# Attention and routing of the second layer in two halves: row sends begin while the second half is still in attention, shared products in waits, and sixteen products of the identity

## The chip, the cores and the metric

The kernel runs on one core of one Trainium2 chip. The metric is the device time of one execution in microseconds (us). Engines are named as in the profile: PE (TensorE), DVE (VectorE), ACT (ScalarE), POOL (GpSimd), SP (SyncE, which issues transfers).

## The reference, cut to what matters

x and ctx hold 8 blocks of 128 tokens with 256 values. Two layers follow one another; each adds an attention and a routed feed-forward network to x. The change concerns what lies between the first network and the second.

```python
h = layernorm(x)                                   # layer 1, attention
theta = theta_w @ ctx; phi, g = phi_w @ h, g_w @ h # 64 latent rows per block
t = softmax(theta^T phi) weighs g                  # 256 x 256 scores per block
z = layernorm over all 64 x 256 values of t, times ln_gamma, plus ln_beta
x = x + ctx + out_w @ relu(z) + out_b

h = layernorm(x)                                   # layer 1, network: 32 experts, top 6
scores = sigmoid(h @ gate_w.T)                     # 8 groups of 4 experts, best 4 groups allowed
idx = top_k(masked scores, 6); w = scores[idx] / sum * 2.5
y = sum over k of w_k * expert_idx_k(h)            # silu(h w11) * (h w33) @ w22
x = x + y + shared(h)                              # one expert twice as wide, for every token
```

Layer 0 has a long convolution as its attention and a network of 8 experts, top 2.

## The kernel before

**Tiling.** All 1024 tokens lie in SBUF as 8 blocks of 128 partitions x 256 values (`x_sb`, normalised `h_sb`, turned `hT_hi` and `hT_lo`, which together hold full precision). Each engine runs its own program; the order of the work is written out by hand in it, and semaphores join them. There is no planner.

**Attention of layer 1.** PE makes theta, phi and g of all blocks, then per block `scores`, `turn_probs` (turning the 256 x 256 probabilities) and `weigh`. DVE takes row maxima (`row_max`, L1301), divides by the sums (`normalise`, L1306 and L1308) and takes statistics of `tx` (L1314). ACT makes the exponentials. The norm over 64 x 256 values goes by groups of four blocks: averages over partitions on PE (`means`, `spreads`), `variance` on DVE, the power -0.5 on POOL (L705), `shifts` on DVE (L1341), scale and shift on ACT; gamma and beta are applied on POOL for blocks 0 to 3 (L711, L717) and on DVE for blocks 4 to 7 (`affine`, L1350, L1352). `outputs` multiplies by out_w, `add_out` (L1360) adds to x.

**Routing of layer 1.** After layer norm 3 of all eight blocks (`veps` L956, power on POOL L588, `shift` L962, normalised rows L976 on DVE and L743 on ACT), PE turns the rows (L1444), makes the logits by expert in eight products of 512 columns (L1454), which ACT copies and PE turns back (L1461). DVE copies scores (L1087), ACT takes the sigmoid, DVE picks groups and experts for all eight blocks (L1092 to L1121). POOL ranks each token's chosen experts by shift and add (`rank` L646, L651, `nth` L656); PE counts rows per expert; DVE makes slots (L1140 to L1153).

**Row sends.** Every token goes to six experts. For k = 0 to 5, DVE stages slots and gates of the k-th choice of all eight blocks (L1211 to L1221), and POOL sends one block of 128 rows at a time to a table `rows_s` in DRAM (L665, an indirect transfer, 48 in all). `staged` has three buffers, so from k = 3 on the staging waits until the sends of k - 3 have landed. POOL's program around it is

```python
pool.wait_ge(slots_made, n * TOPK[0] + k + 1)
for b in range(B):
    ...
    nc.gpsimd.indirect_dma_start(
```

**Experts of layer 1.** 32 chunks of 224 rows: SP loads `rowbuf` from `rows_s` (chunk c waits for the sends of k = 0 to min(c, 5)), PE turns it (L1524) and multiplies (L1431 to L1433, L1557), ACT writes `y_sb` (L840), POOL sends it to a second table `y_s` in two indirect transfers (L683, 64 in all). When these have landed, `y_s` is loaded and added to x, and x is written out. The shared expert's products (`shared_up`, `shared_down`) stand on PE behind the logits. Ahead of the first `turn_rows` PE waits for `add_banks` (L992), which DVE runs behind the last staging.

Of the kernel before, what the change touches and what calls it, by code (L numbers as in the profile page):

```python
# [6 lines left out]
P = 128  # L7
B, S, D = 8, 128, 256
# [41 lines left out]
def build(nc, x_d, ctx_d, ctxr_d, filt_d, skip_d, wr_d, up0_d, down0_d, theta_d, theta_b_d, phi_d, phi_b_d, g_d, g_b_d,  # L50
# [11 lines left out]
    with ExitStack() as stack:  # L62
# [39 lines left out]
        gates = [sb("gates0", [P, B, E0]), sb("gates1", [P, B, E1])]  # L102
        gsum = sb("gsum", [P, B])
        grec = sb("grec", [P, B])
        mask = sb("mask", [P, B, E1])
        rank = [sb(f"rank{i}", [P, B, 16 + E1]) for i in range(2)]
        nth = sb("nth", [P, B, E1])
        cum = [sb(f"cum{i}", [P, 4 + B, E1]) for i in range(2)]
        cend = [sb(f"cend{i}", [P, 16 + E1]) for i in range(2)]
        past = sb("past", [1, MAXC[1] + 2 - FIXED_CHUNKS[1], E1])  # L110
        before = sb("before", [P, P])
        ones = sb("ones", [P, P])
        slot_f = sb("slot_f", [P, B, E1])
        pick = [sb(f"pick{i}", [P, B, E1]) for i in range(2)]
        slot_k = sb("slot_k", [P, B])
        slot_i = sb("slot_i", [P, TOPK1, B], i32)
# [4 lines left out]
        ends_f = sb("ends_f", [1, E1])  # L121
# [31 lines left out]
        idle = sb("idle", [1, 4])  # L153
# [8 lines left out]
        shift2 = sb("shift2", [LAT, B])  # L162
# [55 lines left out]
        pool_made, dve_consts = sem("pool_made"), sem("dve_consts")  # L218
# [10 lines left out]
        lgT_done, lgT_copied, mask_made, ranked = sem("lgT_done"), sem("lgT_copied"), sem("mask_made"), sem("ranked")  # L229
        cum_made = sem("cum_made")  # L230
        nth_made, pool_step = sem("nth_made"), sem("pool_step")
        table_made, h_staged, slots_made = (sem(n) for n in ("table_made", "h_staged", "slots_made"))
        rows_sent = [sem(f"rows_sent{k}") for k in range(TOPK1)]
# [11 lines left out]
        class Ffn:  # L245
# [19 lines left out]
        mean_in, mean_done, dev_in, dev_done, var2_ready, rstd2_ready, shift_made = (sem(n) for n in (  # L265
            "mean_in", "mean_done", "dev_in", "dev_done", "var2_ready", "rstd2_ready", "shift_made"))
        zb_made2 = sem("zb_made2")
        z_made, zg_made, zb_made, relu_made, w_done, ctx_added = (sem(n) for n in (
            "z_made", "zg_made", "zb_made", "relu_made", "w_done", "ctx_added"))
# [62 lines left out]
        def wait_normed(eng, k, batches):  # L332

            eng.wait_ge(normed[1], 6 * k + min(batches, 4) + max(batches - 6, 0))
            if batches > 4:
                eng.wait_ge(normed[0], 2 * k + min(batches - 4, 2))
# [40 lines left out]
        SCORES = (4, 5, 0)  # L377
        OUT = (2, 3, 4, 5)

# [1361 lines left out]
```

## Time and profile before

| | before |
|---|---|
| median of 3 runs | 436.21 us (435.19 to 436.69) |
| the profiled execution's own time | 435.86 us |
| its span in the profile | 434.1 us |
| busy PE / DVE / ACT / POOL | 286.5 / 243.3 / 174.1 / 225.4 us |
| mean granted clock of PE | 0.82 |
| attention of layer 1 starts, about | 184.6 us |
| row sends of layer 1 | 263.9 to 326.8 us |
| y sends of layer 1 | 327.1 to 418.3 us |

The profile is of one execution, 1.76 us shorter in span than its own time. Clock figures are shares of 2.4 GHz, so 0.50 is 1.2 GHz. A timeline row is: start in us, duration in us, engine, line, operation, output <- inputs, shape, count, and in brackets the idle time ahead of it with what ended it.

### The profile page before, as it was taken

Reading aid. Unit: us, or ns where it says so; the run is one execution under the profiler, and the core shown is the slowest. Engines: PE = TensorE matmul, PEld = TensorE weight load, DVE = VectorE, ACT = ScalarE, POOL = GpSimd, SP = SyncE. Lnnn points to the kernel's source line nnn. Section 1 sums busy time; section 2 is a strip of 40 time slices with the busy share of each in tenths; the row PEclk is TensorE's granted clock in tenths of the full one; section 3 lists DMA queues with packets and bytes.
Section 4 is the critical chain, followed back from the end, with each engine's and each line's share of the span. In section 5 each row is a group of like instructions: output and inputs, shape, how many; then the busy total and the mean of one; then the engine's idle time right before and its main releaser. Section 6 shows DMA issues by size and latency. Waiting matters only on the chain.

```text
span 434.1 us, 5040 instructions
## 1 busy us (share of the span) xinstructions
PE 286.5 (66%) x1416; PEld 205.5 (47%) x1416; DVE 243.3 (56%) x659; ACT 174.1 (40%) x378; POOL 225.4 (52%) x253
## 2 busy tenths in 40 slices
PE   0899957202899993299927836621834899998800
PEld 0444433102798881065513524321734899997700
DVE  3599986721353432643667699515412476665467
ACT  2400005501456443254655661201412868886600
POOL 2578821177044654240064045777776667778840
PEclk9999985655999998595975887955866999999955
DMA  7566798424567514999933001343347955699499
GB/s 229 154 169 169 198 298 249 135 99 116 166 198 230 169 45 147 327 321 307 309 116 96 26 1 61 121 144 132 121 144 225 301 164 152 195 293 285 132 376 306
DMA packets 66062, 80.56 MB, mean 186 GB/s; under 512 B 7643, under 2 KB 55061, under 8 KB 66035
## 3 DMA queue, kind: packets, MB, share of 16 engines
q1 hardware_dynamic: 56547, 62.45, 48.9%
q0 software_dynamic: 7296, 16.93, 11.4%
q10 hardware_dynamic: 2192, 0.86, 0.8%
q8 instruction: 12, 0.20, 0.2%
q14 instruction: 15, 0.12, 0.1%
HBM read 43.70 MB, written 38.01 MB: 188 GB/s over the span
## 4 chain that ended last, share of the span: by engine, by line
PE 40%; POOL 18%; DVE 15%; DMA 11%; issue 11%; ACT 4%; SPq 0%; POOLq 0%; DVEq 0%
POOL rows_s L665 12%; PE banks L1557 6%; DMA y_s<-y_sb,place 4%; PE banks L1431 4%; PE banks L1412 3%; PE banks L1432 3%; PE banks L1433 3%; POOL y_s L683 3%; PE banks L1413 3%; PE banks L1414 3%; PE banks L1524 3%; PE banks L1444 2%; PE banks L1644 2%; PE banks L1624 2%; DMA staged<-y_s 2%
## 5 line engine op out<-in xcount | busy, mean ns | idle before, releaser
L683 POOL DMA_INDIRECT y_s<-y_sb,place x88 | 91.0, 1034 | 48.3 <-ACT y_sb L840 24.0
L665 POOL DMA_INDIRECT rows_s<-staged,slot_i x64 | 65.4, 1022 | 28.1 <-issue 27.8
L1431 PE MATMUL banks<-xT_hi,w_hi 128*128 128x224 f32 (+1 forms) x192 | 64.4, 335 | 4.8 <-DVE w_lo L1241 4.5
L1524 PE MATMUL banks<-ident,rowbuf 112*128 112x112 f32 (+1 forms) x176 | 25.7, 278 | 51.1 <-DMA rowbuf<-rows_s 35.6
L1432 PE MATMUL banks<-xT_lo,w_hi 128*128 128x224 f32 (+1 forms) x192 | 57.1, 297 | 0.0
L1433 PE MATMUL banks<-xT_hi,w_lo 128*128 128x224 f32 (+1 forms) x192 | 56.8, 296 | 0.0
L826 ACT ACTIVATE xT_hi<-banks 128x448 fp32r<-128x448 f32 (+1 forms) x40 | 22.9, 574 | 57.3 <-PE banks L1524 55.9
L1557 PE MATMUL banks<-down_raw,hid 128*104 128x256 f32 (+1 forms) x176 | 44.0, 381 | 2.7 <-DVE hid L1263 2.7
L1524 PEld LDWEIGHTS banks<-ident,rowbuf 112*128 112x128 f32 (+1 forms) x176 | 20.1, 153 | 53.3 <-DMA rowbuf<-rows_s 20.8
L1431 PEld LDWEIGHTS banks<-xT_hi,w_hi 128*128 128x128 f32 x192 | 39.0, 203 | 10.3 <-DVE w_lo L1241 7.3
L840 ACT ACTIVATE y_sb<-banks,meta 112x256 f32<-112x256 f32 (+1 forms) x88 | 36.4, 472 | 9.1 <-PE banks L1557 8.7
L743 ACT ACTIVATE h_sb<-x_sb,shift,rstd 128x256 f32<-128x256 f32 x24 | 12.6, 590 | 68.0 <-DVE shift L962 68.0
L1432 PEld LDWEIGHTS banks<-xT_lo,w_hi 128*128 128x128 f32 x192 | 38.9, 203 | 0.8
L1433 PEld LDWEIGHTS banks<-xT_hi,w_lo 128*128 128x128 f32 x192 | 38.9, 202 | 0.0
L604 POOL TENSOR_TENSOR kv<-ctxr_sb 128x512 f32<-128x512 f32 x32 | 32.6, 1043 | 11.4 <-PE banks L1414 11.4
L1233 DVE COPY meta<-rowbuf 112x4 f32<-112x4 f32 (+1 forms) x40 | 7.4, 186 | 50.5 <-ACT xT_hi L826 38.1
L853 ACT ACTIVATE silu_g<-banks 128x224 f32<-128x224 f32 (+1 forms) x48 | 18.3, 382 | 42.4 <-PE banks L1433 42.4
L1557 PEld LDWEIGHTS banks<-down_raw,hid 128*104 128x104 f32 (+1 forms) x176 | 28.0, 172 | 8.3 <-DVE hid L1263 2.9
L1254 DVE COPY place<-meta 112x2 int32<-112x2 int32 (+1 forms) x40 | 7.3, 182 | 35.2 <-DMA y_s<-y_sb,place 18.0
L1236 DVE TENSOR_TENSOR xT_lo<-banks,xT_hi 128x448 fp32r<-128x448 f32 (+1 forms) x40 | 26.1, 653 | 0.0
L588 POOL TENSOR_TENSOR rstd<-veps,minus_half 128x4 f32<-128x4 f32 x8 | 8.5, 1068 | 32.4 <-DVE veps L956 32.4
L1241 DVE TENSOR_TENSOR w_lo<-up_raw,w_hi 128x512 fp32r<-128x512 f32 x36 | 24.4, 681 | 0.0
(221 smaller groups left out, 576.4 us busy)
## 6 DMA issues: line engine op xcount, KB each, us to landing
rows_s<-empty SPq DMA_DIRECT2D x5, 2730.0 KB
up_raw<-in_up SPq DMA_DIRECT2D x38, 256.0 KB, 4.7
rowbuf<-rows_s SPq DMA_DIRECT2D x32, 227.5 KB, 3.5
down_raw<-in_down SPq DMA_DIRECT2D x38, 128.0 KB, 4.3
rows_s<-empty SPq DMA_DIRECT2D x7, 633.8 KB
rowbuf<-rows_s SPq DMA_DIRECT2D x8, 316.9 KB
toep<-filt_s SPq DMA_DIRECT2D x16, 128.0 KB, 3.1
h_sb<-y_s SPq DMA_DIRECT2D x4, 512.0 KB, 4.6
```

Source lines behind the costliest of these rows:

```text
L604: last = nc.gpsimd.tensor_tensor(kv[slot][:, blk].rearrange("p (b i j) -> p b i j", i=HD, j=HD), k, v, ALU.mult)
L665: nc.gpsimd.indirect_dma_start(out=rows_s, out_offset=bass.IndirectOffsetOnAxis(ap=slot_i[:, k, b:b + 1], axis=0), in_=staged[:, b, k % BU ...
L683: nc.gpsimd.indirect_dma_start(out=y_s[n], out_offset=bass.IndirectOffsetOnAxis(ap=place[slot][0:TILE[n], t:t + 1], axis=0), in_=y_sb[slot ...
L826: nc.scalar.activation(xT_hi[par][:, 0:KB * CHUNK[n]].rearrange("p (k c) -> p k c", k=KB), turned(n, par), ACT.Copy)\
L840: last = nc.scalar.activation(y_sb[slot][0:TILE[n], t], y_home(n, slot % 2, t), ACT.Copy, scale=meta[slot][0:TILE[n], t, 0:1])
L1236: nc.vector.tensor_tensor(xT_lo[par][:, cols].rearrange("p (k c) -> p k c", k=KB), turned(n, par), xT_hi[par][:, cols].bitcast(f32).rearra ...
L1241: nc.vector.tensor_tensor(w_lo[slot % 2][:], up_home(n, c, slot), w_hi[slot % 2][:].bitcast(f32), ALU.subtract).then_inc(f.w_split, 1)
L1431: nc.tensor.matmul(out, wh, xh, start=start, stop=False)
L1432: nc.tensor.matmul(out, wh, xl, start=False, stop=False)
L1433: return nc.tensor.matmul(out, wl, xh, start=False, stop=stop)
L1524: last = nc.tensor.transpose(turned(n, slot % 2)[:, k, t * TILE[n]:(t + 1) * TILE[n]], rowbuf[slot][0:TILE[n], t, k * P:(k + 1) * P], iden ...
L1557: last = nc.tensor.matmul(y_home(n, cslot % 2, t), hid[slot % 2][:, t * TILE[n]:(t + 1) * TILE[n]], down_home(n, c, slot), start=first_uni ...
```

## The change

**The same work in another order.** Attention of layer 1 is done for blocks 0 to 3 to its end (phi, scores, weights, both norms, output, layer norm 3), and the routing of these four blocks is put in between the attention work of blocks 4 to 7 on every engine. The list `SENDS` holds all six rounds of half 0, then all six of half 1, four blocks each.

**Other changes.** (1) The norm over `tx` is two operations per block on DVE, `centre` (minus mean, times gamma) and `scale` (times 1/deviation, plus beta); POOL's gamma and beta, ACT's scale and shift, and `shifts` are gone. (2) The logits of layer 1 are made by token, with the turned rows as weights and 64 columns; their copy and turn back are gone. (3) A prefix sum on DVE (`number_half`) takes the place of POOL's ranking in both layers; counts are made from an fp32r mask. (4) `chunk_table` works on 32 partitions. (5) The gates are divided by their sum when they are staged. (6) The shared expert's first products stand ahead of the outputs and turned rows of half 1. (7) `keep_busy` multiplies the identity by itself, ten times ahead of the turned rows of half 1 and six times ahead of its logits; nothing reads the result.

```diff
+        SENDS = [(k, g) for g in range(2) for k in range(TOPK1)]
...
+                else:
+                    for i, (k, g) in enumerate(SENDS):
+                        pool.wait_ge(slots_made, TOPK[0] + i + 1)
+                        for b in range(4 * g, 4 * g + 4):
+                            if k == 0:
+                                pool.wait_ge(h_staged, B + b + 1)
+                            send_rows(k, b)
+
+                            if (i, b) == (0, 3):
+                                power2(1)
+                            if (i, b) == (2, 1):
+                                power_of(3, 1)
...
+            def stage_values(i):
+
+                k, h = SENDS[i]
+                bs = slice(4 * h, 4 * h + 4)
+                if k >= BUFS:
+                    dve.wait_ge(*half_sent(k - BUFS, h))
+                    link(nc.vector.tensor_copy(staged[:, bs, k - BUFS, D + 1].bitcast(i32), ids[:, k - BUFS, bs]))
+                pick_values(1, k, bs, score[:, bs, 0:E1], ROUTE_SCALE)
...
+                    stage_values(6)
+                    shared_hid(1)
+                    stage_values(7)
+                    stage_values(8)
+                    shared_hid(2)
+                    stage_values(9)
+                    shared_hid(3)
+                    stage_values(10)
+                    chunk_table(1, 2)
+                    stage_values(11)
                     add_banks(y_turned, 1, 4)
...
+                def centre(c):
+
+
+                    for b in (2 * c, 2 * c + 1):
+                        last = nc.vector.scalar_tensor_tensor(out=tx[:, b], in0=tx[:, b], scalar=mean_all[:, b:b + 1],
+                                                              in1=gamma_sb[:], op0=ALU.subtract, op1=ALU.mult)
+                    link(last)
...
-                def affine():
...
+                def scale(c):
+                    if c % 2 == 0:
+                        dve.wait_ge(rstd2_ready, c // 2 + 1)
+                    for b in (2 * c, 2 * c + 1):
+                        nc.vector.scalar_tensor_tensor(out=tx[:, b], in0=tx[:, b], scalar=rstd2[:, b:b + 1],
+                                                       in1=beta_sb[:], op0=ALU.mult, op1=ALU.add).then_inc(zb_made, 1)
...
+            def keep_busy(home, count):
+
+
+                for _ in range(count):
+                    nc.tensor.matmul(bank[home][:, 0:P], ident[:], ident[:], start=True, stop=True)
...
+                turn_hidden(1, 0)
+                weigh(5)
+                turn_probs(6)
+                logits(0)
+                turn_probs(7)
+                weigh(6)
+                weigh(7)
+                count_rows(1, slice(0, 4), RANKS[1][0], 2)
                 means(1)
-                pe.wait_ge(tx_copied, B)
                 spreads(1)
-                outputs(0)
-                outputs(1)
+                shared_up(0)
+                output(2)
+                output(3)
+                shared_up(1)
+                keep_busy(2, 10)
+                turn_hidden(1, 1)
+                shared_down(0)
+                keep_busy(6, 6)
+                logits(1)
```

DVE's program for the second half of the attention, which the diff adds, reads (from the layer norm of half 0 on):

```python
variances(3, 0)
normalise(5)
row_max(7)
shifts1(3, 0)
normalise_two((2, 3))
...
sum_logits(0)
choose(0)
...
first_slots(1, slice(0, 4), RANKS[1][0], 4, HALF)
number_half(0)
stage_values(0)
spread_rows(1)
stage_values(1)
centre(2)
variance(1)
centre(3)
stage_values(2)
scale(2)
scale(3)
add_out(2)
add_out(3)
variances(3, 1)
```

**The order on POOL.** These are POOL's instructions from the end of the first network to the y sends of the second, before:

```order
L699 TENSOR_TENSOR x_sb<-x_sb,ctx_sb 128x2048
L705 TENSOR_TENSOR rstd<-veps,minus_half 64x4
L711 TENSOR_TENSOR tx<-tx,gamma_sb 64x512
L705 TENSOR_TENSOR rstd<-veps,minus_half 64x4
L717 TENSOR_TENSOR tx<-tx,beta_sb 64x512
L711 TENSOR_TENSOR tx<-tx,gamma_sb 64x512
L717 TENSOR_TENSOR tx<-tx,beta_sb 64x512
L639 TENSOR_TENSOR w_lo<-up_raw,w_hi 128x512 x2
L588 TENSOR_TENSOR rstd<-veps,minus_half 128x4 x2
L646 COPY rank<-mask 128x8x32
L651 TENSOR_TENSOR rank<-rank 128x8x32 x5
L656 TENSOR_TENSOR nth<-rank,mask 128x256
```

and after the change (L649 is the power of the norm in the attention, L620 that of layer norm 3, L689 a row send, L727 a y send):

```order
L649 TENSOR_TENSOR rstd<-veps,minus_half 64x4
L620 TENSOR_TENSOR rstd<-veps,minus_half 128x4
L689 DMA rows_s<-staged,slot_i 17808x260 x4
L649 TENSOR_TENSOR rstd<-veps,minus_half 64x4
L689 DMA rows_s<-staged,slot_i 17808x260 x6
L620 TENSOR_TENSOR rstd<-veps,minus_half 128x4
L689 DMA rows_s<-staged,slot_i 17808x260 x38
L727 DMA y_s<-y_sb,place 6144x256 x44
```

The ranking and the gamma and beta operations are gone, and half 1's two powers stand behind the fourth and the tenth row send.

**The order on DVE.** This is DVE after the change, from half 1's last scaling of `tx` (L1514) to its turned rows (L1063); L1031 is `veps` of layer norm 3, L1173 to L1180 a staging, L1366 the shared expert's product:

```order
L1514 SCALAR_TENSOR_TENSOR tx<-tx,rstd,beta_sb 64x256 x4
L1522 SCALAR_TENSOR_TENSOR x_sb<-banks,outb_sb,x_sb 128x512
L1022 BN_STATS stats<-x_sb 128x6 x2
...
L1031 TENSOR_SCALAR veps<-mv 128x4
L1359 COPY staged<-ids 128x4
L1173 SCALAR_TENSOR_TENSOR pick<-nth,slot_f 128x128
...
L1180 SCALAR_TENSOR_TENSOR staged<-gate_k,grec 128x4
L1037 SCALAR_TENSOR_TENSOR shift<-mv,rstd 128x4
L1043 TENSOR_SCALAR h_sb<-x_sb,mv,rstd 128x256 x2
L1366 TENSOR_TENSOR hid<-silu_g,up_copy 128x512
L1063 TENSOR_TENSOR hT_lo<-banks,hT_hi 128x512 x2
```

Stagings of half 0 stand between `veps` and `shift` of half 1 and behind `hT_lo`, where before no staging stood ahead of the last logits.

**The order on PE.** This is PE after the change, from the outputs of half 1 (L1911) to its first logits (L1660), without the twelve shared products of `shared_up(1)` between the first two rows:

```order
L1911 MATMUL banks<-tx,outw_sb 128x512 x2
...
L1718 MATMUL banks<-ident 128x128 x10
L1650 MATMUL banks<-ident,h_sb 128x128 x8
L1724 MATMUL banks<-hid,down_raw 128x512 x2
L1718 MATMUL banks<-ident 128x128 x6
L1660 MATMUL banks<-rw,hT_hi 128x64
```

Before, the sixteen turned rows followed the outputs at once, and the eight products of the logits followed these.

## Rows read from the trace of the kernel before

**Rows 1.** The page: the chain that ended last, by line.

```profile
POOL rows_s L665 12%; PE banks L1557 6%; DMA y_s<-y_sb,place 4%; PE banks L1431 4%; PE banks L1412 3%; PE banks L1432 3%; PE banks L1433 3%; POOL y_s L683 3%; PE banks L1413 3%; PE banks L1414 3%; PE banks L1524 3%; PE banks L1444 2%; PE banks L1644 2%; PE banks L1624 2%; DMA staged<-y_s 2%
```

**Rows 2.** Windows by stage: length, busy us of each engine, then PE's granted clock.

```profile
184.60:236.20 51.60, 39.85 (x150) 22.43 (x148) 29.06 (x83) 29.07 (x72) 15.39 (x10) 0.76 0.72 224
236.20:246.60 10.40, 9.64 (x36) 5.80 (x37) 5.54 (x16) 5.98 (x11) 1.01 (x1) 0.67 0.32 109
...
338.30:418.30 80.00, 69.55 (x520) 63.37 (x518) 47.30 (x133) 56.91 (x132) 61.32 (x68) 0.97 0.77 226
418.30:434.10 15.80, 0.00 (x0) 0.00 (x0) 11.21 (x13) 0.00 (x0) 0.00 (x0) 0.50 0.98 328
```

**Rows 3.** Timeline of POOL: row sends (L665) and y sends (L683).

```profile
263.89 1.34 POOL L665 DMA_INDIRECT rows_s<-staged,slot_i  x1 [5.04 <-issue]
...
325.80 0.96 POOL L665 DMA_INDIRECT rows_s<-staged,slot_i  x1 [0.30 <-issue]
327.07 0.97 POOL L683 DMA_INDIRECT y_s<-y_sb,place  x1 [0.30 <-ACT y_sb L840]
...
333.33 0.94 POOL L683 DMA_INDIRECT y_s<-y_sb,place  x1 [0.30 <-issue]
338.31 0.94 POOL L683 DMA_INDIRECT y_s<-y_sb,place  x1 [4.03 <-ACT y_sb L840]
...
417.19 1.11 POOL L683 DMA_INDIRECT y_s<-y_sb,place  x1 [0.30 <-issue]
```

**Rows 4.** DVE's waits from 184.6 to 263.1: total us, times, longest.

```profile
DVE nmax L1301 <- PE banks L1624: 9.8, 7, 3.5
DVE gx L1294 <- PE banks L1614: 5.5, 2, 4.5
```

**Rows 5.** DVE's operations by form, 184.6 to 263.1: busy us, mean ns.

```profile
L984 DVE TENSOR_TENSOR hT_lo<-banks,hT_hi 128x512 fp32r<-128x512 f32 x4 | 2.7, 687 | 1.3 <-ACT hT_hi L780 1.3
L1352 DVE TENSOR_TENSOR tx<-tx,beta_sb 64x512 f32<-64x512 f32 x2 | 2.3, 1162 | 0.1
L1341 DVE SCALAR_TENSOR_TENSOR shift<-mean_all,rstd 64x4 f32<-64x4 f32 x2 | 1.4, 682 | 2.2 <-POOL rstd L705 2.2
L1350 DVE TENSOR_TENSOR tx<-tx,gamma_sb 64x512 f32<-64x512 f32 x2 | 1.4, 680 | 1.2 <-ACT tx L907 1.2
...
L1124 DVE SCALAR_TENSOR_TENSOR gates<-marked,score 128x256 f32<-128x256 f32 x1 | 0.8, 848 | 0.0
...
L1149 DVE SCALAR_TENSOR_TENSOR slot_f<-banks,jump 128x256 f32<-128x256 f32 x1 | 0.4, 425 | 0.0
```

**Rows 6.** Timeline of DVE, from `veps` to the fourth staging.

```profile
237.42 0.17 DVE L956 TENSOR_SCALAR veps<-mv 128x4 f32<-128x4 f32 x1
...
245.72 0.42 DVE L1087 COPY score<-banks 128x256 f32<-128x256 f32 x1 [2.36 <-PE banks L1461]
...
253.16 0.29 DVE L1121 TENSOR_SCALAR mask<-marked 128x256 f32<-128x256 f32 x1
...
262.64 0.42 DVE L1221 TENSOR_REDUCE staged<-pick 128x8 f32<-128x256 f32 x1
...
264.18 0.16 DVE L1163 TENSOR_SCALAR ends_f<-cend 1x32 f32<-1x32 f32 x1
...
270.48 0.40 DVE L1214 SCALAR_TENSOR_TENSOR pick<-nth,slot_f 128x256 f32<-128x256 f32 x1
...
296.50 0.17 DVE L1211 COPY staged<-ids 128x8 int32<-128x8 int32 x1 [7.90 <-DMA rows_s<-staged,slot_i]
```

**Rows 7.** Timeline of PE: two `scores` of one block, and the first chunk's turn.

```profile
195.09 1.99 PE L1624 MATMUL banks<-phT,thT 64*128 64x256 f32 x4
...
210.46 1.13 PE L1624 MATMUL banks<-phT,thT 64*128 64x256 f32 x4
...
301.17 1.75 PE L1524 MATMUL banks<-ident,rowbuf 112*128 112x112 f32 x8 [15.49 <-DVE x_sb L992]
```

**Rows 8.** Timeline of ACT: the first chunk's result.

```profile
310.12 0.84 ACT L840 ACTIVATE y_sb<-banks,meta 112x256 f32<-112x256 f32 x2 [0.51 <-PE banks L1557]
```

More of the change, by code:

```diff
@@ L802, in _, with stage @@
-                for b in range(B):
-                    if n == 1 and b % 2 == 0 and b < 4:
-                        shared_silu(b // 2)
+                def stage(b):
                     copies = min(TOPK[n], BUFS)
@@ new lines, in _ @@
+                normalise_group(2, 0)
+                copy_phi(0)
+                normalise_group(2, 1)
+                copy_phi(1)
+                act.wait_ge(s_up_in, 64)
+                for u in range(2):
+                    nc.scalar.activation(w_hi[u][:], up_raw[u][:], ACT.Copy).then_inc(s_w_hi, 1)
+                for b in range(4):
+                    exps(b)
+                copy_phi(2)
+                copy_pT(0)
+                copy_phi(3)
+                copy_pT(1)
+                copy_tx(0)
@@ new lines, in _ @@
+                stage_next(0)
+                stage_next(1)
+                copy_pT(6)
+                act.wait_ge(normed[0], 8)
+                stage_next(2)
+                sigmoid(0)
+                copy_pT(7)
+                copy_tx(6)
+                stage_next(3)
+                copy_tx(7)
+                load_table(ACT.Silu, 4)
+                rectify(2)
+                rectify(3)
+                shared_silu(0)
+                load_table(ACT.Sigmoid, 5)
+                normalise_group(3, 1)
@@ new lines, in logits_by_expert @@
+            def logits_by_expert(half):
+                pe.wait_ge(hT_lo_made, 2 * half + 2)
+                cols = slice(half * HALF, (half + 1) * HALF)
+                for k in range(KB):
+                    for x in (hT_hi, hT_lo):
+                        last = nc.tensor.matmul(bank[BY_EXPERT[half]][0:2 * E0, :], rw[0][:, k], x[:, k, cols],
+                                                start=(k == 0 and x is hT_hi), stop=(k == KB - 1 and x is hT_lo))
+                last.then_inc(lgT_done, 1)
@@ new lines, in _ @@
+                turn_probs(0)
+                turn_probs(1)
+                phi(2)
+                phi(3)
+                weigh(0)
+                weigh(1)
+                turn_probs(2)
+                turn_probs(3)
+                weigh(2)
+                weigh(3)
+                scores(4)
+                means(0)
+                scores(5)
+                spreads(0)
+                scores(6)
+                make_gx(1)
+                output(0)
+                output(1)
+                turn_probs(4)
```

971 lines of the change are left out of this document (526 added, 445 removed).

## The prediction

> **What bounds the kernel now.** I read the chain of work that ended last first: its largest single line is POOL's row send, 12% of the span [rows 1]. Then the windows by stage: in the 80 us of the experts of layer 1 PE is busy 69.6 us at a granted clock of 0.97, and POOL issues 68 instructions there; in the 51.6 us of the second attention, DVE is busy 29.1 us, POOL 15.4 us and PE 39.9 us, so no engine is full [rows 2]. POOL's timeline gives the skeleton of the end. 48 row sends start at 263.89 and the last at 325.80, 61.9 us for 47 steps, 1.32 each. The first y send starts at 327.07, released by data that ACT had made long before: the first chunk's result was ready at 310.12 + 0.84 = 310.96 [rows 8]. So y sends waited 16 us for POOL's queue alone. After six y sends POOL waits 4.03 us for ACT's next result, then sends at a steady pace: 57 steps from 338.31 to 417.19, 1.384 each [rows 3]. A tail of 15.8 us follows, without PE, ACT or POOL [rows 2]. POOL stands idle while the second attention and its routing run, and afterwards its sends are the bound. What lies ahead of the first row send, and what follows when POOL has it earlier, decide the change.
>
> **The second attention with half 0's routing inside.** From 184.6 to the `veps` of the last half at 237.42 [rows 6] are 52.8 us. Of the 51.6 us to 236.2, 29.1 are DVE's work [rows 2]; with the statistics that follow 30.2, so 22.6 are waits. The largest are those for the scores, 9.8, and for g's product, 5.5 [rows 4].
>
> Removed from DVE: `shifts` 1.4, gamma 1.4, beta 2.3, together 5.1 [rows 5]. `centre` and `scale` are sixteen operations with three inputs on 64 x 256; the nearest row is 128 x 256 in the same form, 0.425 us [rows 5], so 0.4 each, 6.4. Put in ahead of the last `veps`: normalised rows of two blocks, 0.7; two splits of turned rows, 1.4 [rows 5]; score sums and choice for four blocks, half of the 7.4 us between the score copy and the mask [rows 6] plus a fixed part, 4.8; first slots 1.9 and numbering with gate sums 1.7, by their counts of operations at 0.2 to 0.3; three stagings of six operations each, 1.6 each, 4.9. That is 15.4. The work is then 30.2 - 5.1 + 6.4 + 15.4 = 46.9 us.
>
> Of 22.6 us of waits part is filled by this work: half 0's logits, powers and copies now run under half 1's attention and the other way round. But each half is now a chain through PE, ACT and DVE with only four blocks to overlap, and there are new waits for logits, a sigmoid with a table load, and two powers. I take 16 us, between 10 (all of the score and product waits filled but for a few) and 22.6 (none gained). `veps` of half 1 comes at 184.6 + 62.9 = 247.5, ten us later than before; the bounds are 241.5 and 254.
>
> Half 0's first sends leave at about 235, in the middle of this. 24 sends at 1.32 are 31.6 us, with two powers in the queue some 2 more: they end by about 268. This is the lowest start of half 1's sends, whatever DVE does.
>
> **From `veps` to half 1's first send.** Before 26.5 us: 8.3 to the score copy, 7.4 to the mask, 9.5 to the staged gates, then POOL at 263.89 [rows 3, 6]. After: stagings 3 to 5, a shared product and two splits lie between, and PE makes ten and six products of the identity ahead of the turned rows and logits. Four `scores` products of 256 columns take 1.13 us warm and 1.99 cold [rows 7], so one of 128 columns 0.14 to 0.25: the sixteen are 2.3 to 4.0 us, mostly beside the power and the splits; if that cover is gone, all of it delays the logits. I take 0.7 on the path, and 11 us from `veps` to the sums of the logits. Then choice 4.8, numbering 1.7, later slots 4.2, staging 1.6, POOL's wake 0.8: 24.1. Half 1's first send is at 271.6 (T0 below), against 263.9 for the first of all before. But only 24 sends are left then, not 48.
>
> **The experts.** Row sends end at 271.6 + 31.6 = 303.2, 23.6 us earlier. Will a y be ready? DVE's staging 10 waits until eight sends of half 1 have landed. Before, the wait at 296.50 was for 24 sends: the 24th starts at about 294.2, so landing takes 2.4 [rows 3, 6]. Eight are landed at T0 + 11.6; staging 1.8; chunk table 6.3, as between 264.18 and 270.48 [rows 6]; staging 11 1.8; `add_banks` 2.5: the first turn is at T0 + 24. From the first turn at 301.17 [rows 7] to the y at 310.96 [rows 8] are 9.8, and POOL wakes 0.9 later: y sends begin at T0 + 34.8 = 306.4, just behind the row sends. So POOL's queue no longer holds the y sends; they begin 20.7 us earlier. 64 of them at 1.384, the pace that holds with all chunks flowing [rows 3], are 88.6: 395.0. If they kept to six steps of 6.26 us [rows 3], 1.25 each, it would be 80 us; I take the measured long pace, as it contains whatever shares the engine. Then the tail of 15.8 [rows 2]: span 410.8. Before, the same count is 327.1 + 91.2 + 15.8 = 434.1.
>
> The first routing changes little: a scan for POOL's shift and add, one more operation in each staging, +0.3. The profiled execution lies 1.76 above its span and 0.35 under the median: 410.8 + 0.3 + 1.8 + 0.3 = 413.2. **I forecast 413 us**, 23 less.
>
> **The rivals.**
> (a) PE runs at 1.2 GHz through the half-wise stretches. The clock was 0.76 in the attention and 0.67 in the turned rows and logits, with PE busy 9.6 of 10.4 us [rows 2]. A block's `scores` cost 0.86 more cold than warm [rows 7], and its turns and weights as much again and a little more, 2.2; were half of it on the path for eight blocks that is 9, the shared products and logits 4: T0 + 13, time 426. Chance 0.15. The Trainium skill's page "TensorE: Matmul & The Clock Gate", Part 4: PE-mode transpose, says that the faster clock level does not engage for products in transpose mode. By it the turned rows would run at 1.2 GHz whatever stands ahead of them, and ten identity products there would only cost time. The row shows 0.67 over turned rows and logits, which agrees so far as it goes.
> (b) The waits are filled better than I think, and DVE is ready when POOL is. Then T0 is 268 and the y sends keep nearer to 1.25 (64 x 1.25 + 4 for a stall): 302.8 + 84 + 15.8 + 2.4 = 405. Speaking for it: 22.6 us of waits on DVE, none of them with a reason in the data. Against: each half's chain. Chance 0.12.
> (c) Half 0 does not get ahead: its choice or slots wait behind half 1's attention work on DVE, and sends begin after 247 only. Then 48 sends end at 247 + 63 + 5 for gaps = 315, and DVE's later stagings wait for them: the y sends begin at 318 to 327: 425 to 434. Chance 0.09.
> (d) DVE is slowed beside POOL's sends. Beside POOL's ranking the gates product took 0.848, the slot product of the same form with a quiet POOL 0.425 [rows 5]. If a send did the same, the some 15 us of two-input work beside half 0's sends would cost 5 more: 418. Against it: stagings between row sends show 0.40 to 0.42 [rows 6]. Chance 0.03. The Trainium skill's page "GPSIMD Engine Reference", its table of specifications, says that GpSimd shares SBUF interfaces with VectorE, with contention for DVE instructions with two SBUF inputs. The ranking row agrees; that a send counts too no row shows.
> (e) The other side, slower than before: a cycle of waits through POOL's queue. Staging 5 waits for sends 8 to 11, of which the last two stand behind the power that itself needs half 1's last `veps`; DVE stands at staging 5 ahead of the sums of half 1's logits. If the power came late each time, DVE, the sends and PE would go in turn. I find about 2 us of slack there. It costs more than the gain only if T0 comes after 295, 23 us later than worked out. Chance 0.03.
>
> **How the numbers follow.** My own case, 0.58: 408 to 418. The range 404 to 424 takes in (b), (d) and half of (a), and leaves (c), the rest of (a) and (e): about 0.2. Its low end is T0 268 with short steps, its high end T0 + 11. What a measurement of this kernel tells from no change is about 0.3%, 1.3 us. All cases but (e) are faster by more than that, and the top of (c) comes near: faster 0.95, same 0.02, slower 0.03.
>
> **What would show it.** POOL's first row send near 235 and a gap in its sends, then 24 sends without one from about 271; DVE's last `veps` of layer norm 3 near 247; y sends from about 306 with no long wait between the last row send and the first y; 64 of them in 86 to 90 us; the tail unchanged. I am wrong if half 0's first send comes after 245, if the granted clock between 220 and 270 is near 0.5, if y sends begin after 312, or if they take a pace other than 1.38 because PE, no longer with a stock of results, sets it.

## The result, and the profile after

Before 435.73 us (median of 4 runs), after 417.85 us (416.86 to 419.99, 4 runs); the ratio is 0.959, with a 95% interval from 0.955 to 0.964. The kernel became faster by 18 us. The profiled execution after took 417.23 us, with a span of 415.5 us. The unaltered kernel was timed twice more beside the experiments: 415.71 and 416.51 us (medians of 6 runs), ratios 0.955 and 0.956. Ratios leave out the slow runs, those more than 1.5% above the fastest of the same kernel.

The page of after, the chain that ended last by line; it answers to [rows 1]:

```profile
PE banks L1799 8%; POOL rows_s L689 6%; PE banks L1640 5%; PE banks L1641 5%; PE banks L1642 5%; PE banks L1766 4%; PE banks L1621 4%; PE banks L1622 3%; PE banks L1623 3%; POOL y_s L727 3%; DMA y_s<-y_sb,place 2%; DMA staged<-y_s 2%; PE banks L1650 2%; DVE stats L1022 2%; PE banks L1892 2%
```

The share of the row sends fell from 12% to 6%, and PE's last product of the experts (L1799, before L1557) moved to the head of the chain with 8%. The windows of after; they answer to [rows 2]:

```profile
184.60:253.00 68.40, 52.52 (x197) 31.95 (x196) 48.32 (x167) 32.44 (x77) 20.37 (x17) 0.75 0.65 210
...
247.50:253.00 5.50, 5.50 (x9) 2.57 (x9) 3.38 (x10) 2.84 (x5) 4.28 (x5) 0.50 0.34 121
253.00:263.60 10.60, 10.19 (x68) 8.63 (x67) 7.72 (x29) 5.11 (x8) 8.49 (x9) 0.95 0.25 88
...
321.00:397.80 76.80, 69.05 (x519) 63.14 (x517) 45.75 (x132) 56.52 (x132) 59.33 (x68) 0.97 0.77 227
397.80:415.50 17.70, 0.00 (x0) 0.00 (x0) 12.46 (x14) 0.00 (x0) 0.02 (x1) 0.50 0.95 316
```

From 184.6 us to the last `veps` DVE is busy 48.3 of 68.4 us, where it was 30.2 of 52.8. The clock is 0.50 through the outputs of half 1 and 0.95 through its turned rows and logits. POOL's timeline of after, which answers to [rows 3]:

```profile
239.58 1.05 POOL L689 DMA_INDIRECT rows_s<-staged,slot_i  x1 [21.93 <-DVE staged L1180]
...
253.33 1.17 POOL L620 TENSOR_TENSOR rstd<-veps,minus_half 128x4 f32<-128x4 f32 x1
...
271.48 0.96 POOL L689 DMA_INDIRECT rows_s<-staged,slot_i  x1 [0.30 <-issue]
277.15 1.15 POOL L689 DMA_INDIRECT rows_s<-staged,slot_i  x1 [4.71 <-DVE staged L1180]
...
306.98 0.96 POOL L689 DMA_INDIRECT rows_s<-staged,slot_i  x1 [0.30 <-issue]
312.40 0.97 POOL L727 DMA_INDIRECT y_s<-y_sb,place  x1 [4.46 <-ACT y_sb L867]
...
396.88 0.94 POOL L727 DMA_INDIRECT y_s<-y_sb,place  x1 [0.30 <-issue]
```

Half 0's 24 sends run from 239.6 to 272.4 with nothing but the two powers between them; POOL then waits 4.71 us for half 1's first staging, and the second 24 sends end at 307.9 instead of 326.8. The first y send waits for ACT now, 4.46 us, where before it waited for POOL's queue. DVE's and PE's timelines of after, which answer to [rows 6] and [rows 7]:

```profile
232.38 0.23 DVE L1314 TENSOR_SCALAR mask_r<-marked 128x128 fp32r<-128x128 f32 x1
...
237.10 0.29 DVE L1173 SCALAR_TENSOR_TENSOR pick<-nth,slot_f 128x128 f32<-128x128 f32 x1
...
240.15 0.29 DVE L1173 SCALAR_TENSOR_TENSOR pick<-nth,score 128x128 f32<-128x128 f32 x1
...
253.03 0.22 DVE L1031 TENSOR_SCALAR veps<-mv 128x4 f32<-128x4 f32 x1
...
263.58 0.41 DVE L1284 TENSOR_REDUCE pick<-banks 128x128 f32<-128x256 f32 x1
...
288.70 0.17 DVE L1359 COPY staged<-ids 128x4 int32<-128x4 int32 x1 [2.58 <-DMA rows_s<-staged,slot_i]
```

```profile
220.27 1.97 PE L1650 MATMUL banks<-ident,h_sb 128*128 128x128 f32 x8
...
247.16 3.78 PE L1911 MATMUL banks<-tx,outw_sb 64*128 64x512 f32 x4 [2.56 <-ACT tx L932]
...
255.16 2.39 PE L1718 MATMUL banks<-ident 128*128 128x128 f32 x20
257.39 1.04 PE L1650 MATMUL banks<-ident,h_sb 128*128 128x128 f32 x8
258.26 1.88 PE L1724 MATMUL banks<-hid,down_raw 128*128 128x512 f32 x4
259.98 1.50 PE L1718 MATMUL banks<-ident 128*128 128x128 f32 x12
...
301.66 1.75 PE L1766 MATMUL banks<-ident,rowbuf 112*128 112x112 f32 x8 [10.36 <-DVE x_sb L1071]
```

The mask of half 0's choice is at 232.38, the last `veps` at 253.03, the first row send of half 1 (T0) at 277.15: 24.1 us behind the `veps`. The ten identity products take 2.2 us until the turned rows begin, the six 1.3. The profile counts each identity product twice (x20 and x12); each turned row is counted once. The first turn of a row buffer is at T0 + 24.5 and the first y send at T0 + 35.3.

### The profile page after: what moved, and what is told of

Same layout as the page of the kernel before. It is cut to its first block, busy times and chain, and to the rows that moved or that the text cites. A ratio compares the mean times of both kernels' runs of the same rounds, so it can differ in the third digit from the quotient of the medians.

```text
span 415.5 us, 5260 instructions
## 1 busy us (share of the span) xinstructions
PE 290.9 (70%) x1479; PEld 213.6 (51%) x1479; DVE 257.5 (62%) x757; ACT 170.0 (41%) x372; POOL 211.5 (51%) x239
## 4 chain that ended last, share of the span: by engine, by line
PE 45%; DVE 20%; POOL 11%; DMA 10%; issue 8%; ACT 5%; SPq 0%; POOLq 0%; DVEq 0%
PE banks L1799 8%; POOL rows_s L689 6%; PE banks L1640 5%; PE banks L1641 5%; PE banks L1642 5%; PE banks L1766 4%; PE banks L1621 4%; PE banks L1622 3%; PE banks L1623 3%; POOL y_s L727 3%; DMA y_s<-y_sb,place 2%; DMA staged<-y_s 2%; PE banks L1650 2%; DVE stats L1022 2%; PE banks L1892 2%
## 5 line engine op out<-in xcount | busy, mean ns | idle before, releaser
L727 POOL DMA_INDIRECT y_s<-y_sb,place x88 | 90.2, 1025 | 48.1 <-ACT y_sb L867 24.2
L689 POOL DMA_INDIRECT rows_s<-staged,slot_i x64 | 64.1, 1001 | 62.5 <-DVE staged L1180 44.1
L1640 PE MATMUL banks<-xT_hi,w_hi 128*128 128x224 f32 (+1 forms) x192 | 63.3, 330 | 4.9 <-DVE w_lo L1405 4.7
L1641 PE MATMUL banks<-xT_lo,w_hi 128*128 128x224 f32 (+1 forms) x192 | 56.0, 292 | 0.0
L1642 PE MATMUL banks<-xT_hi,w_lo 128*128 128x224 f32 (+1 forms) x192 | 55.9, 291 | 0.0
L1766 PE MATMUL banks<-ident,rowbuf 112*128 112x112 f32 (+1 forms) x176 | 24.8, 271 | 31.1 <-DMA rowbuf<-rows_s 20.7
L1799 PE MATMUL banks<-down_raw,hid 128*104 128x256 f32 (+1 forms) x176 | 44.0, 381 | 0.9 <-DVE hid L1427 0.8
L1640 PEld LDWEIGHTS banks<-xT_hi,w_hi 128*128 128x128 f32 x192 | 37.9, 197 | 10.2 <-DVE w_lo L1405 6.5
L767 ACT ACTIVATE h_sb<-x_sb,shift,rstd 128x256 f32<-128x256 f32 x22 | 11.7, 590 | 69.5 <-DVE shift L1037 69.5
L1641 PEld LDWEIGHTS banks<-xT_lo,w_hi 128*128 128x128 f32 x192 | 38.0, 198 | 0.8
L1642 PEld LDWEIGHTS banks<-xT_hi,w_lo 128*128 128x128 f32 x192 | 37.9, 197 | 0.0
L1799 PEld LDWEIGHTS banks<-down_raw,hid 128*104 128x104 f32 (+1 forms) x176 | 28.0, 173 | 6.6 <-DVE hid L1427 1.2
L620 POOL TENSOR_TENSOR rstd<-veps,minus_half 128x4 f32<-128x4 f32 x8 | 8.7, 1085 | 37.4 <-DVE veps L1031 37.4
L1400 DVE TENSOR_TENSOR xT_lo<-banks,xT_hi 128x448 fp32r<-128x448 f32 (+1 forms) x40 | 26.1, 653 | 0.0
```

The costliest lines, as they stand in the source:

```text
L689: nc.gpsimd.indirect_dma_start(out=rows_s, out_offset=bass.IndirectOffsetOnAxis(ap=slot_i[:, k, b:b + 1], axis=0), in_=staged[:, b, k % BU ...
L727: nc.gpsimd.indirect_dma_start(out=y_s[n], out_offset=bass.IndirectOffsetOnAxis(ap=place[slot][0:TILE[n], t:t + 1], axis=0), in_=y_sb[slot ...
L1400: nc.vector.tensor_tensor(xT_lo[par][:, cols].rearrange("p (k c) -> p k c", k=KB), turned(n, par), xT_hi[par][:, cols].bitcast(f32).rearra ...
L1640: nc.tensor.matmul(out, wh, xh, start=start, stop=False)
L1641: nc.tensor.matmul(out, wh, xl, start=False, stop=False)
L1642: return nc.tensor.matmul(out, wl, xh, start=False, stop=stop)
```

## The experiments

Single executions of this kernel differ by up to 5 us (412.5 to 417.6 in one of the further series), and part of that arises ahead of half 0's mask, where no version has an edit that the mask waits for. So each run is read first by three distances in its own trace: from the mask of half 0 to the last `veps` (20.7 us in after), from there to T0 (24.1), and from T0 to the first y send (35.3). The two further traces of the unaltered kernel gave 19.9 and 20.7, 24.1 and 24.0, 35.0 and 35.3. Each trace is of one execution, so a difference no larger than that between these three is not a finding. Times come second, as ratios to before; for the unaltered kernel these were 0.959, 0.955 and 0.956.

**Half 0's sends not ahead.** This asks whether the gain is the early sends or one of the other edits.

```diff
-                stage_values(0)
                 spread_rows(1)
-                stage_values(1)
...
                 later_slots()
+                for i in range(6):
+                    stage_values(i)
...
+                    power2(1)
+                    power_of(3, 1)
                     for i, (k, g) in enumerate(SENDS):
```

> After with half 0's six stagings moved behind half 1's slots and both powers ahead of the first row send, so that no row is sent while half 1's attention goes on; all else as in after, half 0's choice and slots too. Theory (all of the gain is that 24 of 48 sends go out beside half 1's attention): first send at about 268 to 270, 48 of them at 1.29, the last ends at about 331, y sends from 332, time 438 to 442, the gain gone. Rival (part of the gain is in the other edits, scan, norm on DVE, logits by token, shared products in waits): time 425 to 433.

Measured: 438.70 us, ratio 1.010 (1.004 to 1.016), against 415.71 of the unaltered kernel on the same chip. POOL's timeline:

```profile
268.79 1.05 POOL L689 DMA_INDIRECT rows_s<-staged,slot_i  x1 [20.28 <-DVE staged L1178]
...
328.96 0.96 POOL L689 DMA_INDIRECT rows_s<-staged,slot_i  x1 [0.30 <-issue]
...
334.24 0.97 POOL L725 DMA_INDIRECT y_s<-y_sb,place  x1 [4.32 <-ACT y_sb L865]
```

The first send is 29 us later than in after, 8 us earlier than its T0, and the last sends end 22 us later. The theory holds: sending 24 of 48 blocks beside half 1's attention is worth 23 us, and all the rest of the change together, the price of halving the attention included, gives nothing: this version is 0.4 to 1.6% slower than before. What each of the other edits gives or takes by itself was not run.

The trace shows the price of the early stagings too. Without them the last `veps` comes 15.6 us behind half 0's mask instead of 20.7, and DVE's work up to it is 43.4 us instead of 48.3: stagings 0 to 2 cost DVE 4.9 us there, and none of that lay in its waits.

**The power further back in POOL's queue.**

```diff
-                            if (i, b) == (2, 1):
+                            if (i, b) == (3, 1):
                                 power_of(3, 1)
```

> After with half 1's layer norm power behind the fourteenth row send instead of the tenth. Theory (POOL's queue holds what stands behind sends; each costs 1.27): the power starts 5 us later than its veps allows, T0 is 4 to 5 us later relative to the last veps, the time 4 to 5 longer. Rival (DVE fills the wait with stagings and the row sends are bound by POOL's own total): T0 1 to 2 later, time within 1.5 us.

Measured: 422.63 us, ratio 0.971 (0.966 to 0.976), 6.1 us above the unaltered kernel on that chip. POOL, then DVE:

```profile
256.28 0.96 POOL L689 DMA_INDIRECT rows_s<-staged,slot_i  x1 [0.30 <-issue]
257.27 1.04 POOL L620 TENSOR_TENSOR rstd<-veps,minus_half 128x4 f32<-128x4 f32 x1
...
264.96 0.96 POOL L689 DMA_INDIRECT rows_s<-staged,slot_i  x1 [4.14 <-DVE staged L1180]
```

```profile
258.34 0.16 DVE L1037 SCALAR_TENSOR_TENSOR shift<-mv,rstd 128x4 f32<-128x4 f32 x1 [4.40 <-POOL rstd L620]
```

The `veps` was ready at 251.92; the power starts 5.4 us later and T0, at 280.43, is 28.5 behind the `veps` instead of 24.1. DVE idles 4.40 us, then stages late, and POOL idles 4.14 us in its turn. So the queue is a real price, 4.4 us for four sends, and in the changed kernel the power does stand where it costs nothing: there it starts 0.3 us after the start of its `veps`, and `shift` follows the staging without a wait. The theory holds. The rest of the 6.1 us is not accounted for; T0 to the first y send is 36.5 here, 1.2 more than in after.

**Half 1's norm ahead of half 0's stagings.** This tests why the last `veps` is late.

```diff
                 first_slots(1, slice(0, 4), RANKS[1][0], 4, HALF)
+                spread_rows(1)
                 number_half(0)
+                variance(1)
                 stage_values(0)
-                spread_rows(1)
-                stage_values(1)
                 centre(2)
-                variance(1)
                 centre(3)
-                stage_values(2)
                 scale(2)
                 scale(3)
+                stage_values(1)
...
+                    power2(1)
                     for i, (k, g) in enumerate(SENDS):
...
-                            if (i, b) == (2, 1):
+                            if (i, b) == (1, 2):
```

Stagings 2, 3 and 5 stand one place further back each, behind the last `veps`, the shared product and the logit sums. POOL's first power goes ahead of the first send, the second behind the seventh.

> After with half 1's norm over the latent rows put ahead of half 0's first staging and sends: spread_rows behind the slots, variance ahead of staging 0, centre and scale ahead of staging 1, the power ahead of the first send, the other power behind the seventh. Theory (half 0's routing on DVE is what makes half 1's last veps late): that veps comes 3.5 to 4 us earlier, at about 249.3, T0 at about 274.3 where POOL's own queue becomes the bound, time 415 (-2.5 to -3). Rival: the waits on PE and ACT take over and veps moves by less than 1.5 us; time 417 to 418.

Measured: 414.77 us, ratio 0.953 (0.948 to 0.958). Its `veps` and sends, on DVE and POOL:

```profile
231.72 0.23 DVE L1313 TENSOR_SCALAR mask_r<-marked 128x128 fp32r<-128x128 f32 x1
...
247.31 0.17 DVE L1030 TENSOR_SCALAR veps<-mv 128x4 f32<-128x4 f32 x1
```

```profile
239.10 1.05 POOL L689 DMA_INDIRECT rows_s<-staged,slot_i  x1 [0.72 <-DVE staged L1179]
...
272.74 1.15 POOL L689 DMA_INDIRECT rows_s<-staged,slot_i  x1 [2.39 <-DVE staged L1179]
```

Mask to `veps` fell from 20.7 to 15.6 us. T0 gained less, 3.7 us against the mask, since the stagings that were passed over now lie behind the `veps`: 25.4 instead of 24.1. The theory holds: half 0's numbering and its first three stagings, where they stood in DVE's program, were 5 us of the lateness. One part of it failed: T0 was to be bound by POOL's own queue, but POOL still waited 2.39 us for DVE's staging. The time alone would not show the gain, as the interval overlaps those of the unaltered kernel (0.955 to 0.964, 0.949 to 0.960, 0.951 to 0.962); the distance does.

**Chunk table earlier.**

```diff
-                    stage_values(10)
                     chunk_table(1, 2)
+                    stage_values(10)
```

> After with the chunk table made ahead of staging 10 instead of behind it. DVE waits 2.6 us for sends ahead of staging 10, and the table fits there. Theory: PE's first turn of a row buffer is held by DVE's last work, so it comes at 299.1 instead of 301.7, the first y send at 309.9 instead of 312.4, and the time falls by 2.5 us to 415.3. Rival: the row sends, which end at 307.9 in any case, and the later pace of the y sends set the end, and the time moves by less than 1 us.

Measured: 417.83 us, ratio 0.958 (0.952 to 0.964). PE and POOL:

```profile
302.74 1.76 PE L1766 MATMUL banks<-ident,rowbuf 112*128 112x112 f32 x8 [7.76 <-DVE x_sb L1071]
```

```profile
280.82 1.16 POOL L689 DMA_INDIRECT rows_s<-staged,slot_i  x1 [3.65 <-DVE staged L1180]
...
310.59 1.51 POOL L689 DMA_INDIRECT rows_s<-staged,slot_i  x1 [0.30 <-issue]
314.57 0.97 POOL L727 DMA_INDIRECT y_s<-y_sb,place  x1 [2.47 <-ACT y_sb L867]
...
401.42 1.35 POOL L727 DMA_INDIRECT y_s<-y_sb,place  x1 [0.31 <-issue]
```

The first turn is at T0 + 21.9 instead of 24.5, as the theory said, but the first y send only at T0 + 33.8 instead of 35.3. From its start to the start of the last one are 86.9 us instead of 84.5, and the span ends at T0 + 137.6, where the three traces of the unaltered kernel have 138.4, 136.2 and 137.8. Of the 2.6 us at the head nothing is left at the end that can be told. My theory for this run falls, its rival holds.

**Without the sixteen products of the identity.**

```diff
-                keep_busy(2, 10)
                 turn_hidden(1, 1)
                 shared_down(0)
-                keep_busy(6, 6)
                 logits(1)
```

> After without its sixteen products of the identity. Theory of the prediction: they are mostly beside other work and cost about 0.7 us on the path, so without them the time falls by 0 to 1 us. Rival, from the trace of after: PE ran the turned rows in 1.04 us and each product of the logits in 0.11 at the fast clock level right behind them, where half 0's turned rows without them took 1.97; without them PE is slow there, T0 (half 1's first row send) comes 1 to 2.5 us later than 277.2, and the time rises by as much, to 419 to 420.

Measured: 418.43 us, ratio 0.959 (0.954 to 0.965), no difference from the unaltered kernel that can be told. PE:

```profile
257.82 1.21 PE L1650 MATMUL banks<-ident,h_sb 128*128 128x128 f32 x8
258.87 1.88 PE L1724 MATMUL banks<-hid,down_raw 128*128 128x512 f32 x4
...
261.31 0.28 PE L1660 MATMUL banks<-rw,hT_lo 128*128 128x64 f32 x1
261.42 0.28 PE L1660 MATMUL banks<-rw,hT_hi 128*128 128x64 f32 x1
```

Without them the turned rows take 1.21 us instead of 1.04, and the logits go at the same 0.11 from start to start. `veps` to T0 is 23.8 us instead of 24.1. PE reached its fast level without them: granted 0.50 up to 257.4, while `shared_up(1)` ran, and 0.84 over the turned rows. The rival that I wrote falls: the identity products are not needed for it, and up to T0 they cost 0.3 us where the prediction had put 0.7, no more than traces of one kernel differ by. Behind T0 this execution lost time: the first y send came at T0 + 37.3 instead of 35.3, after DVE had waited 3.98 us instead of 2.58 for landed sends ahead of staging 10. Whether that belongs to the edit or to this one execution the run does not show.

**The shared products back behind the counts.** The complement: the identity products stay and the shared expert's first products go back, and with them the two table loads that they need on ACT.

```diff
-                shared_up(0)
                 output(2)
                 output(3)
-                shared_up(1)
                 keep_busy(2, 10)
                 turn_hidden(1, 1)
-                shared_down(0)
                 keep_busy(6, 6)
                 logits(1)
...
                 if n == 1:
+                    shared_up(0)
+                    shared_up(1)
+                    shared_down(0)
                     shared_up(2)
```

> After with the shared expert's first products undone alone: they stand behind the last counts again, and the table loads that they need on ACT are gone with them; the identity products stay. Theory (they only fill waits, and moved back they fill the wait for the rows of the experts, in which PE is busy 12 of 24 us): within 1 us of the control, or up to 3 longer, because the chain of silu, product and copy on three engines grows by one half. Rival (they were what kept PE at the fast level ahead of the turned rows and logits): T0 1.5 to 3 us later relative to the last veps, 24.1 in after, and the time up by that too.

Measured: 414.81 us, ratio 0.955 (0.950 to 0.961), against 416.51 and 0.956 of the unaltered kernel on that chip: no difference. `veps` at 249.62 to T0 at 273.19 is 23.6 us, T0 to the first y send 34.6, and the logits run 0.11 apart here too:

```profile
243.75 3.78 PE L1912 MATMUL banks<-tx,outw_sb 64*128 64x512 f32 x4 [7.34 <-ACT tx L933]
...
256.24 0.28 PE L1658 MATMUL banks<-rw,hT_lo 128*128 128x64 f32 x1
256.35 0.28 PE L1658 MATMUL banks<-rw,hT_hi 128*128 128x64 f32 x1
```

So PE is at the fast level at the logits with either the shared products or the identity products alone, and neither moves the time. What happens without both was not run.

**Ten more identity products ahead of the outputs of half 1.**

```diff
                 shared_up(0)
+                keep_busy(2, 10)
                 output(2)
                 output(3)
```

> After with ten more products of the identity in PE's wait ahead of the outputs of half 1. In after these outputs took 3.78 us at the slow clock level, half 0's 1.98. Theory (the slow level there is part of why veps was late): outputs take 1.9 to 2.5, T0 0.8 to 1.8 earlier, time down by as much. Rival: the ten products run slowly themselves and hold the outputs up by up to 2 us, time up by 1 to 2.

Measured: 415.49 us, ratio 0.955 (0.950 to 0.960). PE:

```profile
242.76 2.66 PE L1718 MATMUL banks<-ident 128*128 128x128 f32 x20
245.35 1.98 PE L1911 MATMUL banks<-tx,outw_sb 64*128 64x512 f32 x4
```

The same row in the first further trace of the unaltered kernel:

```profile
250.40 2.08 PE L1911 MATMUL banks<-tx,outw_sb 64*128 64x512 f32 x4 [1.93 <-ACT tx L932]
```

The outputs took 1.98 us instead of 3.78, but they began 15.6 us behind half 0's mask instead of 14.8, directly behind the added products. Mask to `veps` is 20.4 instead of 20.7. But the unaltered kernel's outputs took 2.08 us as well in another execution, beginning 15.2 us behind the mask, and mask to `veps` was 19.9 there. So the short outputs can't be put down to the added products; what the row does show of these is that the outputs waited for them. The two traces of the unaltered kernel with outputs of 3.78 us have 20.7, the one with 2.08, and that with the chunk table earlier (2.09), 19.9: the level is worth some 0.8 us at the `veps`, less than the 1.7 to 1.8 by which the outputs are shorter, because DVE waits for the first output alone. The ratio cannot be told from the unaltered kernel's 0.955 to 0.959.

**Both moves together, and both without the identity.** The first has the edits of the norm and of the table, of which the cut shows the table's and one of POOL's; the second leaves out the two `keep_busy` lines too.

```diff
+                    power2(1)
                     for i, (k, g) in enumerate(SENDS):
...
+                    chunk_table(1, 2)
                     stage_values(10)
-                    chunk_table(1, 2)
                     stage_values(11)
```

> The norm of half 1 ahead of half 0's stagings, and the chunk table ahead of staging 10, together. If they add: 2.5 to 3.5 us from the first and 1 from the second, 413.5 to 414.5. If the table gives nothing once it is beside the row sends' end: 414.5 to 415.5, as the first alone.

> As the kernel with both moves, and without the sixteen identity products. Theory from the run without them (they stand ahead of PE's logits for 0.4 us and the products behind shared_up run at the fast level anyway): 0 to 0.5 us faster than with them, 413 to 414.5. Rival: with half 1's norm moved ahead PE is idle longer before the turned rows, runs them slowly, and the time is 1 to 2 us longer.

> The changed kernel once more, unaltered, beside the others of this call. It gives what two runs of one kernel differ by. Any theory: 416.5 to 419.

> The changed kernel once more, unaltered, on the chip of the two others of this call. Any theory: 415 to 419.

Measured: 412.99 us, ratio 0.951 (0.946 to 0.956); without the identity 411.87 us, ratio 0.950 (0.945 to 0.955); the unaltered kernel beside them 415.71, and on a third chip 416.51. DVE with the identity:

```profile
257.30 0.43 DVE L1283 TENSOR_REDUCE pick<-banks 128x128 f32<-128x256 f32 x1 [1.35 <-PE banks L1659]
```

DVE and POOL of the one without it:

```profile
245.30 0.41 DVE L1030 TENSOR_SCALAR veps<-mv 128x4 f32<-128x4 f32 x1
...
253.70 0.42 DVE L1283 TENSOR_REDUCE pick<-banks 128x128 f32<-128x256 f32 x1 [0.15 <-PE banks L1659]
```

```profile
267.42 1.00 POOL L689 DMA_INDIRECT rows_s<-staged,slot_i  x1 [0.30 <-issue]
269.24 1.16 POOL L689 DMA_INDIRECT rows_s<-staged,slot_i  x1 [0.82 <-DVE staged L1179]
```

`veps` to the logit sums takes 8.4 us here and 10.8 with the identity (from 246.46 to 257.30). In this order one staging instead of two lies between DVE's last split and the sums; with the identity DVE has to wait 1.35 us for the logits, without it 0.15, and T0 is 23.9 us behind the `veps` instead of 26.1. So the cover of the identity products is gone, and they are on the path, as the prediction had said of that case. POOL's gap between the halves is down to 0.8 us: T0 (269.24) is nearly bound by POOL's own queue, as the prediction's low end had it. The time is not at that end, because from the first y send to the end of the last are 88.9 us. The interval doesn't separate this version from the one with the identity, and it overlaps that of the unaltered kernel beside it (0.949 to 0.960) a little; its median is 3.8 us under the unaltered kernel's on the same chip, and it is the lowest of all that were run.

## Why the prediction was right, and where it was off

The forecast was 413 with a range of 404 to 424; the time is 417.85, inside it, and so are 415.71 and 416.51. The mechanism was right; one term was 5.5 us too small, and two at the end took part of it back. By its own steps, the forecast span 410.8 against 415.5 measured:

- **Half 0's sends beside half 1's attention are the gain**: right, shown by the run without them. They begin at 239.6, not 235, and end at 272.4, not 268.
- **`veps` of half 1 at 247.5**: this is the term that was mis-sized. It measured 253.0, 5.5 late (252.5 and 255.1 in the further traces). DVE's work was forecast at 46.9 us and is 48.3. The rest are waits, 20.1 us against the 16 that I chose between 10 and 22.6; 1.0 of them is that the attention began 1.0 later than in the trace of before. The prediction had put the first routing at 0.3, and its first row send did move from 86.59 to 87.45, but in the further traces it came at 86.10 and 84.78, so no lateness of that part is shown. Of the 9.8 us that DVE had waited for the scores 1.8 are left, so those waits were filled, as forecast. What the prediction took too low is the new waits of a chain of four blocks: ACT's copies of `tx` 5.8 us, the outputs 2.3, and the sigmoid 2.1, which stood behind ACT's copies of rows to be sent and not, as the prediction has it, behind its table load. The runs without early stagings and with the norm first show that 5 us of the lateness is half 0's work on DVE where it stands in the order.
- **24.1 us from `veps` to T0**: measured 24.12, and 23.98 and 24.11 in the two further runs. The exact agreement is luck in part: the terms measured 10.6, 5.1, 2.2, 4.3, 1.7 and 0.3 against 11, 4.8, 1.7, 4.2, 1.6 and 0.8. The identity products were forecast at 0.7 on the path; the trace without them has 0.3 less.
- **24 sends in 31.6 us**: measured 30.8 from 277.15 to 307.94.
- **First turn at T0 + 24, first y send at T0 + 34.8**: measured 24.5 and 35.3. That POOL's queue no longer holds the y sends is right: POOL waits 4.46 us for the first y.
- **64 y sends in 88.6 us**: measured 85.4, and 85.7 and 86.8 in the further traces. POOL's gaps beyond the usual 0.3 us between two sends sum to 3.0 us, against 4.5 in the stretch of before from which the pace was taken, and its long sends took less as well. Thirteen gaps end with ACT's result, but eleven of them are 0.3 us long, as any gap is, so waiting for a result cost little: PE makes a chunk every 2.59 us, POOL's two sends take 2.5, and the two are about level.
- **Tail 15.8 us**: measured 17.7, at a DMA share of 0.95. This is one execution's: the further traces have 15.5 and 15.7. So the forecast of an unchanged tail holds.

T0 + 5.55, first y + 0.45, y sends - 3.2, tail + 1.9 makes 4.7: 410.8 + 4.7 = 415.5.

Two of the signs by which the prediction would call itself wrong showed. The y sends were not to begin after 312; they began at 312.4, and at 314.2 and 311.8 in the further traces, nearly all of the lateness being T0's. And their pace was not to differ from 1.38 because PE sets it; it is 1.34, and PE is level with POOL there. The range held because it had room for a late T0, not because every step was right.

Of the rivals, (a), PE at the slow level, is true in part: the outputs ran at 0.50, and in the attention the clock was 0.75 as before (0.76). It did not reach half 1's logits. In the first 34 us of the attention it did cost time, as the last section shows. The page "TensorE: Matmul & The Clock Gate" of the Trainium skill, Part 4: PE-mode transpose, has the fast level not engage for turned rows. Here eight turned rows took 1.04 us at 257.39, in a stretch granted 0.95, and 1.97 at 220.27, where the grant was 0.50, so the measurement goes against it. That the identity products ahead of them would only cost time came out all the same: without them the turned rows took 1.21 us, and the time did not change. (b), the filled waits, is false for the kernel as changed; with both moves and no identity T0 was 269.2, near its 268, but the time 411.9 and not 405. (c) is false: half 0's sends began 37.6 us ahead of T0. (d) is false: the product of a staging takes 0.29 us at 237.10, ahead of the first send, and 0.29 at 240.15, beside it. (e) is false: DVE runs from staging 4 to staging 5 without a wait. That such a cycle could be built is shown by the power behind the fourteenth send.

## What to carry to other kernels

When one engine's serial queue (here 48 transfers of 1.3 us) follows a long stage in which that engine is idle, look for the half of the work that can be made ready early: its worth is the time that the queue is busy beside the other stage, less what the split adds to the slowest engine of that stage. Within a half-wise order, what stands on the busiest engine ahead of the second half's last link can cost its full length, as the three stagings here did (4.9 us of work, 5.1 us of delay); put there only as much as keeps the queue fed. Do not count on an engine's waits to take up added work: here DVE's work up to the last `veps` grew from 30.2 to 48.3 us, and its waits only shrank from 22.6 to 20.1, since a chain over fewer blocks has waits of its own.

## What the runs showed of the hardware

The clock that PE was granted in one stretch differs between executions of one and the same program. In after it was 0.80 from 184.6 to 219.0 us, in a further run of the same kernel 0.65, and in the kernel with the additional identity products, whose code in that stretch is the same, 0.95. Between the two levels of 1.2 and 2.4 GHz (0.50 and 1.00), such a mean says for what part of the stretch PE had the fast one. The windows of the further run, and its PE timeline:

```profile
184.60:219.00 34.40, 33.38 (x109) 21.24 (x108) 19.56 (x49) 14.34 (x41) 8.35 (x4) 0.65 0.97 298
```

```profile
185.10 3.78 PE L1866 MATMUL banks<-phT,thT 64*128 64x256 f32 x8
```

In after these eight products took 1.99 us. From the start of this attention (here DVE's first normalised rows, 184.87 in after) to half 0's mask, the versions below differ in nothing that the mask waits for, so the distance shows what the level costs:

| trace | granted clock, 184.6 to 219.0 | start | half 0's mask | distance, us |
|---|---|---|---|---|
| first further run | 0.65 | 183.49 | 235.22 | 51.7 |
| chunk table earlier | 0.65 | 185.28 | 237.02 | 51.7 |
| after | 0.80 | 184.87 | 232.38 | 47.5 |
| second further run | 0.80 | 183.08 | 231.81 | 48.7 |
| ten more identity products | 0.95 | 184.10 | 229.71 | 45.6 |
| shared products back | 0.95 | 182.97 | 228.57 | 45.6 |

The level in these 34 us moves the mask by 6 us, more than most edits tried here. It is one source of the spread of 5 us in the time of one kernel and not the only one: the first further run reached its mask 2.8 us later than after did, and its span was 415.4 against 415.5, with a tail shorter by 2.2. Why the level differs was not found.
